# Second attention layer of a graph network: sums over edge lists by target tile, instead of dense strips of weights

## The reference

```python
xr = jnp.einsum('nd,rdf->rnf', x, W)
oi = xr[etype, dst]
oj = xr[etype, src]
qi = oi @ q
kj = oj @ k
alpha = jax.nn.leaky_relu(qi + kj, NEG_SLOPE)
m = jax.ops.segment_max(alpha, dst, num_segments=n_nodes)
e = jnp.exp(alpha - m[dst])
z = jax.ops.segment_sum(e, dst, num_segments=n_nodes)
a = e / (z[dst] + EPS)
msg = (a[:, :, None] * oj.reshape(-1, heads, out_ch)).reshape(-1, heads * out_ch)
out = jax.ops.segment_sum(msg, dst, num_segments=n_nodes)
return out + b
```

## Time and profile before

| | us |
|---|---|
| runs: median of 3 (lowest to highest) | 1804.38 (1795.9 to 1808.99) |
| profiled execution: time | 1802.21 |
| its span | 1800.4 |
| PE busy | 1602.7 (89%) |
| DVE busy | 1240.6 (69%) |
| ACT busy | 580.6 (32%) |
| POOL busy | 97.9 (5%) |
| transfers, 297.79 MB, share of 16 DMA engines on the main queue | 53.6% |
| mean granted TensorE clock | 0.938 of 2.4 GHz |

### The profile page before, as it was taken

One profiled execution on the slowest core, in us unless ns is written; L12 is line 12 of the kernel. 1 busy time (PEld: TensorE's weight loads), 2 busy tenths in 40 slices (PEclk: granted clock), 3 DMA queues, 4 the chain that ended last, 5 costly groups with the idle time before them and its releaser, 6 DMA issues. The chain is left out here.

```text
span 1800.4 us, 27904 instructions
## 1 busy us (share of the span) xinstructions
PE 1602.7 (89%) x10121; PEld 1406.6 (78%) x10121; DVE 1240.6 (69%) x1980; ACT 580.6 (32%) x876; POOL 97.9 (5%) x58
## 2 busy tenths in 40 slices
PE   5999887887878899989979997969999999999996
PEld 4675354544538799989979997966999989999996
DVE  7346766656426998999999899953564275746773
ACT  2332122222312353344335434423222132223522
POOL 1000000000003000400220040000000000000000
...
GB/s 210 226 242 143 14 81 81 70 99 96 79 162 189 186 180 208 186 185 194 154 166 226 186 157 154 139 71 201 215 247 199 234 159 203 225 156 203 204 211 78
DMA packets 175212, 297.79 MB, mean 165 GB/s; under 512 B 35306, under 2 KB 117612, under 8 KB 174580
## 3 DMA queue, kind: packets, MB, share of 16 engines
q1 hardware_dynamic: 174996, 296.04, 53.6%
...
q10 hardware_dynamic: 96, 0.12, 0.0%
...
## 5 line engine op out<-in xcount | busy, mean ns | idle before, releaser
L1089 PE MATMUL ah_ps<-ah_xr,ah_T 125*125 125x194 f32 x2400 | 405.7, 332 | 40.3 <-issue 37.1
L1089 PEld LDWEIGHTS ah_ps<-ah_xr,ah_T 125*125 125x125 f32 x2400 | 402.2, 191 | 42.8 <-issue 37.9
L1664 PE MATMUL sl_ps<-sl_masks,sl_wH 125*125 125x256 f32 x1800 | 322.9, 282 | 11.0 <-DVE sl_wL L1504 10.1
L1664 PEld LDWEIGHTS sl_ps<-sl_masks,sl_wH 125*125 125x125 f32 x1800 | 275.6, 187 | 13.2 <-DVE sl_wL L1504 6.9
L921 ACT ACTIVATE ah_T<-ah_T,ah_kq 125x625 f32<-125x625 f32 x240 | 195.9, 817 | 223.1 <-DVE ah_T L1019 223.1
L1664 PE MATMUL sl_ps<-sl_masks,sl_wL 125*125 125x256 f32 x900 | 253.7, 282 | 0.0
L1002 DVE CUSTOM_DVE_ANT_0 ah_dump<-ah_krow,ah_gap 125x1250 bf16<-125x1250 f32 x120 | 206.1, 1781 | 15.6 <-DMA ah_krow<-ah_d_k 15.5
L1019 DVE SCALAR_TENSOR_TENSOR ah_T<-ah_rows,ah_k_rest 125x625 f32<-125x625 f32 x240 | 211.5, 883 | 0.4
L1026 DVE SCALAR_TENSOR_TENSOR ah_T<-ah_T,ah_cnt 125x625 f32<-125x625 f32 x240 | 192.9, 804 | 19.3 <-DMA ah_cnt<-d_C 17.6
L1664 PEld LDWEIGHTS sl_ps<-sl_masks,sl_wL 125*125 125x125 f32 x900 | 168.5, 187 | 0.0
L610 PE MATMUL fr_ps<-fr_col_hot,fr_row_hot 125*128 x516 | 123.8, 367 | 44.6 <-DVE fr_col_hot L404 37.7
...
## 6 DMA issues: line engine op xcount, KB each, us to landing
...
sl_d_xr<-sl_xs SPq DMA_DIRECT2D x60, 384.0 KB, 3.7
...
fr_raw<-in_w SPq DMA_DIRECT2D x36, 384.0 KB, 5.9
...
```

The source lines that it names most:

```text
L1089: mm = pe.matmul(o, T[:, g % TR, t * P:(t + 1) * P], xr[:, r, j], start=(first and t % 2 == 0), stop=final, skip_group_check=True)
L1664: mm = pe.matmul(flat[:, u * TW:(u + 1) * TW], a[:, i % AR, ts], xr[:, i % LR, x, fs], start=(first and u % 2 == 0 and q == 0), stop=(last ...
```

## The change

In the front, the loads of the residual rows and the stores of x1 are made in parts of 112 and 13 rows (`PARTS`), two transfers for one.

A new stage, `edge_lists`, stands between the heads and the second layer, in a block of its own. It loads the ids of the edges (125 x 160) again and makes a list in which the edges of one target tile stand together, filled up to pairs of 128-slot chunks: 88 pairs, 176 chunks (`NPAIR`, `NCH`). DVE compares and scans to find each edge's slot; for each of 160 columns of ids DVE makes three one-hots (128, 176 and 176 columns, fp16) and PE multiplies them (352 columns), so that each slot receives its source and its key. From them come, per slot, the row to gather (`edge_row`), the target in the tile (`slot_dst`), the relation (`rel_hot`), an empty mark, and per pair its target tile (`pair_tile`); the targets also go to DRAM (`d_dl`).

In `second_layer` head and transform stay. The transformed row is stored once in full fp32 (no high and low part), 386 columns a half: 384 features, a one (for the sum of weights) and the k logit; DVE's subtraction per unit is gone. Beside the last 22 units, for 8 chunks each: SP loads the slots' targets spread over the partitions (`load_dst`, 512 KB), DVE compares them with the row number (`hot_rows`, 125 x 1024), PE picks for each slot its target's q logits less the maximum (`pick`: 8 products of 6 columns in fp32, behind a load of 4 tile numbers into registers), DVE takes them over (`take_picked`).

The strips are replaced. POOL gathers for each of 176 chunks 128 rows of 772 fp32 by indirect DMA into the room of hH and hL (4 x 4 chunks), after all stores and all transform products; further ones wait for the pair that used the room. DVE computes the logits of four chunks (`alpha`, `larger`), ACT the exp, DVE the one-hots with the weight in them (`weighted_hot`, 128 x 125), PE multiplies (`pair`: 2 chunks x 2 halves, 386 columns, operands in fp32, not fp32r), and DVE adds each pair's 772 columns to its target tile in SBUF (`add_pair`, tile number from a register). The tail of all ten tiles stands after the last pair.

```diff
+NPAIR = (E + NT * (2 * CH - 1)) // (2 * CH)
+NCH = 2 * NPAIR
...
-                sp.dma_start(d_x1[n * P:(n + 1) * P, :], v_sb[:, n % VR]).then_inc(out_done[n % VR], 16)
+                for p0, pn in PARTS:
+                    sp.dma_start(d_x1[n * P + p0:n * P + p0 + pn, :], v_sb[p0:p0 + pn, n % VR]).then_inc(out_done[n % VR], 16)
...
+def edge_lists(kit, keep, lists, src_t, dst_t, ety_t, d_dl):
...
+            rounded(tile[:], idf[:, 1], 1.0 / P, 0.5 / P - 0.5)
+            link(v.scalar_tensor_tensor(out=local[:], in0=tile[:], scalar=-float(P), in1=idf[:, 1], op0=ALU.mult, op1=ALU.add))
+            link(v.scalar_tensor_tensor(out=key[:], in0=idf[:, 2], scalar=float(CH), in1=local[:], op0=ALU.mult, op1=ALU.add))
+            link(v.tensor_scalar(key[:], key[:], 1.0, None, ALU.add))
+            link(v.tensor_tensor(hot[:], io_f[0:P, 0:NT].rearrange("p (t o) -> p t o", o=1).to_broadcast([P, NT, ET]),
+                                 tile[:].rearrange("p (o c) -> p o c", o=1).to_broadcast([P, NT, ET]), ALU.is_equal))
+            v.wait_ge(starts_set, 2)
+            link(v.tensor_tensor_scan(run[:].rearrange("p t c -> p (t c)"), starts[:].rearrange("p t c -> p (t c)"),
+                                      hot[:].rearrange("p t c -> p (t c)"), 0.0, ALU.mult, ALU.add))
+            v.tensor_copy(total[:], run[:, :, ET - 1]).then_inc(total_made, 1)
+            v.wait_ge(sums_done, 1)
+            rounded(pairs[:], ps[0:P, 1, NT:2 * NT], 1.0 / (2 * CH), 0.5 - 0.25 / CH)
...
+            link(v.tensor_tensor(run[:], run[:], base[:].rearrange("p (t o) -> p t o", o=1).to_broadcast([P, NT, ET]), ALU.add))
+            link(v.tensor_tensor(run[:], run[:], hot[:], ALU.mult))
+            link(v.tensor_reduce(pos[:], run[:].rearrange("p t c -> p c t"), AX.X, ALU.add))
+            for c in range(ET):
+                if c >= KR:
+                    v.wait_ge(hot_used, c - KR + 1)
+                v.tensor_scalar(lo_hot[:, c % KR], io[0:P, 0:CH], lo[:, c:c + 1], None, ALU.is_equal).then_inc(hot_made, 1)
+                v.tensor_scalar(hi_val[:, c % KR, 0], io[0:P], hi[:, c:c + 1], idf[:, 0, c:c + 1], ALU.is_equal, ALU.mult)\
+                 .then_inc(hot_made, 1)
+                v.tensor_scalar(hi_val[:, c % KR, 1], io[0:P], hi[:, c:c + 1], key[:, c:c + 1], ALU.is_equal, ALU.mult)\
+                 .then_inc(hot_made, 1)
...
+                pe.wait_ge(hot_made, 3 * (c + 1))
+                mm = pe.matmul(ps[:, 0, 0:2 * NCH], lo_hot[:, c % KR], hi_val[:, c % KR].rearrange("p a n -> p (a n)"),
+                               start=(c == 0), stop=(c == ET - 1))
...
+            def load_dst(g):
+                if g >= 2:
+                    sp.wait_ge(hot_T_made, g - 1)
+                sp.dma_start(dst_row[:, g % 2], d_dl[g * PW:(g + 1) * PW].rearrange("(o n) -> o n", o=1).to_broadcast([CH, PW]))\
+                  .then_inc(dst_row_in[g % 2], 16)
...
+            for i in range(XR):
+                pool.wait_ge(xs_out[i], 32 * len([k for k in range(NU) if k % XR == i]))
+            pool.wait_ge(xr_done, NU)
+            for c in range(NCH):
+                if c >= 4 * QR and c % 2 == 0:
+                    pool.wait_ge(pair_done, (c - 4 * QR) // 2 + 1)
+                pool.indirect_dma_start(slot(c).rearrange("p a d -> p (a d)"), None, d_xr,
+                                        bass.IndirectOffsetOnAxis(ap=edge_row[:, c:c + 1], axis=0)).then_inc(gathered[c // 4 % QR], 16)
...
+            def hot_rows(g):
+                v.wait_ge(dst_row_in[g % 2], 16 * (g // 2 + 1))
+                if g == 0:
+                    v.wait_ge(iotas, 2)
+                if g >= 2:
+                    v.wait_ge(picked_done, g - 1)
+                v.tensor_scalar(hot_T[:, g % 2], dst_row[0:P, g % 2], io_p[:], None, ALU.is_equal).then_inc(hot_T_made, 1)
...
+            def alpha(q):
+                cs = slice(4 * q, 4 * q + 4)
+                v.wait_ge(gathered[q % QR], 64 * (q // QR + 1))
+                if q >= 2:
+                    v.wait_ge(exped, q - 1)
+                k = slots(q)[:, :, 1, FW + 1]
+                v.scalar_tensor_tensor(out=al[:, q % 2, 1], in0=k, scalar=SLOPE, in1=rqe[:, cs, 1], op0=ALU.mult, op1=ALU.add)\
+                 .then_inc(chain, 1)
+                n_links[0] += 1
+                link(v.tensor_tensor(al[:, q % 2, 0], k, rqe[:, cs, 0], ALU.add))
+            def larger(q):
+                v.tensor_tensor(al[:, q % 2, 0], al[:, q % 2, 0], al[:, q % 2, 1], ALU.max).then_inc(alpha_made, 1)
+            def weighted_hot(c):
+                if c % 4 == 0:
+                    v.wait_ge(exped, c // 4 + 1)
+                if c >= SR:
+                    v.wait_ge(pair_done, (c - SR) // 2 + 1)
+                v.tensor_scalar(hot[:, c % SR], io_f[:], slot_dst[:, c:c + 1], ex[:, c:c + 1], ALU.is_equal, ALU.mult)\
+                 .then_inc(hot_made, 1)
+            def add_pair(p, t):
+                v.wait_ge(pair_done, p + 1)
+                v.wait_ge(added, p)
+                a = acc[:, bass.ds(t, 1)].rearrange("p o a d -> p (o a) d")
+                v.tensor_tensor(a, a, ps[0:P, 2 * (p % 4):2 * (p % 4) + 2, 0:SW], ALU.add).then_inc(added, 1)
...
+            for q in range(NQ + 2):
+                if q < NQ:
+                    alpha(q)
+                    larger(q)
+                if 1 <= q <= NQ:
+                    for c in range(4 * q - 4, 4 * q):
+                        weighted_hot(c)
+                if q >= 2:
+                    p = 2 * (q - 2)
+                    if p % 8 == 0:
+                        ts = tiles_of(p, 8, DVE)
+                    for i in range(2):
+                        add_pair(p + i, ts[(p + i) % 8])
+                if q % 4 == 3 and q // 4 < NT:
...
+            def pick(g):
+                pe.wait_ge(hot_T_made, g + 1)
+                if g == 0:
+                    pe.wait_ge(rq_made, 2)
+                    pe.wait_ge(kqT_copied, 3)
+                ts = tiles_of(g * PIECE // 2, PIECE // 2, PE)
+                for i in range(PIECE):
+                    c = g * PIECE + i
+                    bank = pick_bank(c)
+                    o = (c - BANKS[bank][0]) * 2 * R
+                    mm = pe.matmul(ps[:, 4 + bank, o:o + 2 * R], hot_T[:, g % 2, i * CH:(i + 1) * CH],
+                                   rq[:, bass.ds(ts[i // 2], 1)].rearrange("p o a r -> p (o a r)"), start=True, stop=True)
+                mm.then_inc(picked_done, 1)
+            def pair(p):
+                if p == 0:
+                    pe.wait_ge(xs_made, 2 * NU)
+                    pe.wait_ge(rqe_made, 1)
+                if p >= 4:
+                    pe.wait_ge(added, p - 3)
+                for c in (2 * p, 2 * p + 1):
+                    pe.wait_ge(hot_made, c + 1)
+                    for a in range(2):
+                        mm = pe.matmul(ps[0:P, 2 * (p % 4) + a, 0:SW], hot[:, c % SR], slot(c)[:, a], start=(c % 2 == 0),
+                                       stop=(c % 2 == 1))
+                mm.then_inc(pair_done, 1)
...
+                if PICK_AT < k:
+                    pick(k - PICK_AT - 1)
+            pick(NG_T - 1)
+            for p in range(NPAIR):
+                pair(p)
...
+        edge_lists(kit, keep, lists, src_t, dst_t, ety_t, d_dl)
+        kit.end_stage()
+        second_layer(kit, keep, lists, d_h, wqk2, d_gap, w2, b2, d_x1, out, d_dl)
```

553 lines of the change are left out of this document (256 added, 297 removed).

## The result

The changed kernel takes 1910.5 us (median of 4 runs, 1909.1 to 1912.4), the kernel before 1803.4 in the same comparison: ratio 1.060, 95% interval 1.056 to 1.064. The direction and the range were right; the likeliest time, 1872, was 38.5 us too low. The profiled execution has a span of 1907.2 us, clock 0.900, against the forecast span of 1870.6: 36.6 us to find.

The account below looks back on a forecast made before the run. PE sets the pace in the second layer's two long stretches; front -2.0, list stage +102.5, picks +34.9, strips to pairs -80.4 and tail +15.2 sum to +70.2 us, giving 1872 us; range 1840 to 1950.

Parts of the forecast that it names:

- (a): Front: x1 transfers in 112 and 13 rows instead of 125 shorten the change-over to the next stage, -2.0 us.
- the fourth rival: Front loop: x1's slow transfers hold it up, so the split returns up to 57 us, giving 1815; chance 0.03.
- (b): New list stage between heads and second layer, behind a barrier with PE idle: +102.5 us, 69 of it one-hots.
- the 49 us: List stage: what the one-hots would come to by the skill's four-columns-a-cycle rule, making the kernel 20 us less.
- The third rival: List stage: the one-hots don't overlap, 0.69 us a column of ids for 0.43, 110 for 69, 1913; chance 0.08.
- (c): Picks inside the transform: small PE products with no idle time to put them in, register loads taken as 0; +34.9 us.
- (d): Second layer: strips out -333.3, ramp +18.3, 88 PE-paced pairs +231.6, slow clock +3; together -80.4 us.
- the +3 for the clock: Start of the pairs: PE starts after idling, with the granted clock near the 1.2 GHz level; +3 us.
- the 1.32 from which it sticks out: Pairs: POOL's issue time per gather, in us, from which it is no longer hidden beside PE's 2.63 a pair.
- the first rival: Pairs: POOL's gather issue is the bound; at 1.6 us each 1922, at 2.11 2012; chance 0.25.
- The second rival: Pairs: POOL works only when DVE rests, 4.3 us a pair, 2018, or 2.8 and 1887 by the skill's page; chance 0.05.
- (e): Tail: ten tiles instead of five end after the last product, takes 2.8 us apart, 35.6 against 20.4; +15.2 us.

Follow-up runs that it names:

- g_poolplain: The changed kernel with the front's step numbers cut to 16 bits (1922.0 us), its gathers made as plain loads of 128 consecutive rows by POOL: 1892.2 us.

## Why the prediction was right, and where it was off

**(a) The front: wrong in size, -2.0 for -15.3.** The change-over came out as forecast, 7.4 us from the last x1 product to the next stage before, 5.4 after. But the fourth rival, which I gave 0.03, was true in part: the transfers of 125 rows did hold up the loop. I dismissed it because no row named a DMA; the 56.6 us of "issue" on DVE in the earlier trace rows were where it stood, and I read them as the price of register loads, not as something that a transfer lengthens. The step that failed is the -2.0, which counts only the last transfer's own landing.

**(b) The list stage: the mechanism was right, a term was mis-sized.** The term is "0.15, 0.15 and 0.13 = 0.43" a column of ids: 0.235, 0.235 and 0.163. The step that failed is the reading of the earlier trace rows. I divided the whole pace of a 750-column comparison, 0.39 us, by its columns and took the 1.92 columns a ns for the rate, with some 0.06 us of fixed time on top. In truth 0.19 us of the 0.39 is fixed with two scalars from SBUF and 0.20 is the stream. At 176 columns the fixed part is four fifths. The same misreading made me set the rule on four columns a cycle of the Trainium skill (the page named above) aside. Its rate was right, but the 49 us that I worked out with it would have been further off, since the fixed part stayed at 0.06. The third rival, 110 us for no overlap, came near the measured 101 by luck: the three do overlap (means of 325, 325 and 254 ns, 0.634 us for all).

**(c) The picks: right.** The register loads cost nothing visible, as taken: no wait of PE names them. The pass was 0.106 instead of 0.117, which gives 22 x 16 x 0.011 = 4 us back. What I had not costed is the zeroing, 6.5 us of DVE work before the first comparison: 5.8 us of waiting and 4 at the slower clock. "ACT and DVE have slack" was true over the stage and false at that place.

**(d) Ramp right to 0.2 us; the pairs' price right, their flow not.** The pass was 0.328 us in g_poolplain (231 us for 704, the slow start included, so the +3 for the clock came on top of a price that already held), the gather's issue 1.25 us for the 1.2 taken, under the 1.32 from which it sticks out. So the first rival, POOL as the bound, did not come true as it stands; that POOL has next to no time to catch up may well have made the stalls dearer. What I had no rival for is a signal that is seen late: 23 us more than forecast, 26 to 27 as against the pairs of the runs without the indirect form. The transfers were never the bound (plain loads of the same bytes hide). The second rival, POOL against DVE, is not what happened either: DVE's own operations have their length throughout, 954 ns an addition with the gathers and 957 without.

**(e) The tail: right**, the takes are 2.68 apart for the 2.8 taken.

**The whole.** "The pairs save 80 us on PE's path, and lists, picks and tail cost 153" is by measurement: strips out 333.3, ramp and pairs in 275.8, so 57 saved, against 131.6 + 39.9 + 13.6 = 185, less 21 in front, heads and the layer's head. The sign never hung on the mis-sized terms. That the total is off by 37 us and not by more than 50 is luck: the list stage, the pairs and the transform were 57 too cheap, and a front that I had dismissed, with small gains elsewhere, gave 21 back.
